# Where the gate's sigmoid is taken: moved from ScalarE's eviction to a pass over the reloaded gate, in a linear-attention layer on eight cores

## The reference, cut to what matters

```python
xn = layernorm(x)
# attention half, 16 heads of 128, blocks of 256 tokens
q, k, v = split(silu(xn @ w_qkv.T))
# per head, over the 8 blocks:
o_inter = (q * q_decay) @ kv
o_intra = ((q @ k.T) * diag_decay) @ v
kv      = block_decay * kv + (k * k_decay).T @ v
out  = norm_w * out * rsqrt(mean(out * out) + 1e-6)     # over all 2048 features
gate = sigmoid(xn @ w_gate.T)
s    = (gate * out) @ w_out.T
# weight of the second half, from 4 planes of 2048x2048 each
W    = sum_n (sigmoid(pw_n) - sigmoid(nw_n)) * c_n
g    = silu(xn @ W.T + bias)
y    = x + s * g
```

## Time and profile before

| | us |
|---|---|
| median of 2 runs | 2446.24 (2442.86 to 2449.62) |
| the profiled execution, whole | 2436.33 |
| its span, slowest core (core 5) | 2434.5 |
| spans of the 8 cores | 2415.6 to 2434.5 |
| busy on core 5: TensorE, VectorE, ScalarE | 1639.0, 868.0, 569.7 |

### The profile page before, as it was taken

One profiled execution on the slowest core, in us unless ns is written; L12 is line 12 of the kernel. 1 busy time (PEld: TensorE's weight loads), 2 busy tenths in 40 slices (PEclk: granted clock), 3 DMA queues, 4 the chain that ended last, 5 costly groups with the idle time before them and its releaser, 6 DMA issues.

```text
span 2434.5 us, 22652 instructions; the slowest of 8 cores (2415.6 to 2434.5 us)
## 1 busy us (share of the span) xinstructions
PE 1639.0 (67%) x7928; PEld 765.6 (31%) x7928; DVE 868.0 (36%) x1613; ACT 569.7 (23%) x827; POOL 191.1 (8%) x308
## 2 busy tenths in 40 slices
PE   1110545554459999288888888888888887357896
PEld 1110212221124444144344343434334343123332
DVE  5555254445550000223333333333333333623455
ACT  1225355555562122311111111111111111000000
POOL 0002232222220000000000000000000000110000
PEclk9999777776679999699999999999999998578998
DMA  8219899999991111122222212222222200697554
GB/s 190 101 55 121 118 158 154 155 162 161 152 156 37 39 37 56 23 27 44 44 44 44 35 30 32 35 44 44 44 44 44 44 18 9 130 190 168 169 166 154
DMA packets 176704, 211.74 MB, mean 87 GB/s; under 512 B 74064, under 2 KB 123216, under 8 KB 172496
## 3 DMA queue, kind: packets, MB, share of 16 engines
q0 software_dynamic: 135936, 109.07, 35.4%
q1 hardware_dynamic: 40656, 101.23, 12.7%
HBM read 277.37 MB, written 41.94 MB: 131 GB/s over the span
## 4 chain that ended last, share of the span: by engine, by line
PE 46%; DMA 27%; DVE 12%; issue 8%; ACT 5%; SPq 2%; DVEq 0%; POOL 0%; ACTq 0%; POOLq 0%
PE pfA L579 29%; DMA pnbg<-nwT 19%; DMA xT_fc<-xT 6%; PE pfA L452 5%; PE pS L452 5%; ACT sq_b L724 2%; DVE sT_b L675 2%; PE pT L611 2%; SPq L841 1%; DVE mneg_c L197 1%; DVE s L910 1%; DVE s L916 1%; PE pS L727 1%; DMA xtile<-x 1%; PE pS L663 1%
## 5 line engine op out<-in xcount | busy, mean ns | idle before, releaser
L579 PE MATMUL pfA<-xnT,wq_sb 128*128 128x512 bf16 x3072 | 721.4, 390 | 46.0 <-ACT q_dim L595 43.0
L579 PEld LDWEIGHTS pfA<-xnT,wq_sb 128*128 128x128 bf16 x3072 | 298.5, 100 | 404.5 <-issue 83.9
L354 PE MATMUL pfA<-xnT,wg_sb 128*128 128x512 bf16 x512 | 146.5, 457 | 307.1 <-ACT gate_stA L364 245.5
L675 DVE TENSOR_TENSOR sT_b<-pS,decT_all 128x512 bf16<-128x512 f32 x128 | 88.4, 690 | 317.6 <-PE pS L663 317.6
L406 DVE TENSOR_TENSOR sgp<-sgp,sgn 128x1024 bf16<-128x1024 bf16 x128 | 88.6, 692 | 269.8 <-ACT sgn L402 269.8
L354 PEld LDWEIGHTS pfA<-xnT,wg_sb 128*128 128x128 bf16 x512 | 57.1, 114 | 396.1 <-issue 358.4
L732 DVE SCALAR_TENSOR_TENSOR O_st<-pO,csb,gate_h 128x256 bf16<-128x256 f32 x128 | 61.9, 483 | 308.0 <-ACT sq_b L724 306.4
L397 ACT ACTIVATE sgp<-pnbg 128x1024 bf16<-128x1024 bf16 x128 | 135.2, 1056 | 133.5 <-DMA pnbg<-pwT 125.7
L402 ACT ACTIVATE sgn<-pnbg 128x1024 bf16<-128x1024 bf16 x128 | 135.1, 1056 | 91.5 <-DMA pnbg<-nwT 86.1
L901 PE MATMUL pfA<-O_sb,wout_sb 128*128 128x512 bf16 x512 | 125.7, 404 | 31.9 <-DVE s L910 31.9
L901 PE MATMUL pS<-O_sb,wout_sb 128*128 128x512 bf16 x512 | 119.7, 393 | 25.6 <-DMA O_sb<-o_scr 15.9
(11 more groups left out here) (106 smaller groups left out, 1491.9 us busy)
## 6 DMA issues: line engine op xcount, KB each, us to landing
pnbg<-pwT POOLq DMA_DIRECT2D x128, 256.0 KB, 14.1
pnbg<-nwT POOLq DMA_DIRECT2D x128, 256.0 KB, 13.2
wq_sb<-wqkvT POOLq DMA_DIRECT2D x16, 1536.0 KB, 19.2
xtile<-x SPq DMA_DIRECT2D x16, 1024.0 KB, 5.4
xT_fc<-xT SPq DMA_DIRECT2D x16, 1024.0 KB, 7.5
outT<-outb SPq DMA_DIRECT2D x64, 256.0 KB, 2.4
wg_sb<-wgateT POOLq DMA_DIRECT2D x16, 512.0 KB, 15.3
gate_scr<-gate_stA SPq DMA_DIRECT2D x16, 512.0 KB, 9.3
```

Source lines behind the costliest of these rows:

```text
L354: r = e.matmul(pbank[:], wg_sb[b][:, fc * HD:(fc + 1) * HD], xnT[:, fc * T + tg * 512: fc * T + tg * 512 + 512], start=(fc == 0), stop=(fc ...
L579: r = e.matmul(pfA[par][:], wq_sb[hb][:, fc * 384 + sel * 128: fc * 384 + (sel + 1) * 128], xnT[:, fc * T + tg * 512: fc * T + tg * 512 + ...
L675: tst = sch.op("V", (lambda h, jp: lambda e: e.tensor_tensor(out=sT_b[:, jp * 512:(jp + 1) * 512], in0=pS[jp][:], in1=decT_all[:, h * 512: ...
```

## The change

The eviction of the gate's matmuls in stage B moves from ScalarE to VectorE and becomes a plain copy; DRAM then holds the gate before its sigmoid. In stage C a sigmoid is taken in place over the whole tile `gate_h` (128x2048) on ScalarE, after each load: twice ahead of the loop (heads 0 and 1), and 14 times at a head boundary. The multiplication L732 waits for that instead of for the load.

```diff
-                tok_gst[h * NTG + tg] = sch.op("S",
-                    (lambda h, gb, tg, pbank: lambda e: e.activation(
-                        out=gate_st[gb][:, tg * 512:(tg + 1) * 512], in_=pbank[:],
-                        func=AF.Sigmoid))(h, gb, tg, pbank),
+                tok_gst[h * NTG + tg] = sch.op("V",
+                    (lambda h, gb, tg, pbank: lambda e: e.tensor_copy(
+                        out=gate_st[gb][:, tg * 512:(tg + 1) * 512],
+                        in_=pbank[:]))(h, gb, tg, pbank),
                     waits=[tok_gmm[(h, tg)], tok_gsd.get(h - 1)], inc=True)
...
+        tok_gsig[0] = sch.op("S", lambda e: e.activation(
+            out=gate_h[0][:], in_=gate_h[0][:], func=AF.Sigmoid),
+            waits=[tok_gld[0]], inc=True)
...
+            tok_gsig[1] = sch.op("S", lambda e: e.activation(
+                out=gate_h[1][:], in_=gate_h[1][:], func=AF.Sigmoid),
+                waits=[tok_gld[1]], inc=True)
...
                 waits=[tog, t_cst, tok_ost.get(h - 2), tok_sq[(h, j)],
-                       tok_gld[h]], inc=True)
+                       tok_gsig[h]], inc=True)
...
+                    tok_gsig[sh + 2] = sch.op("S",
+                        (lambda sh: lambda e: e.activation(
+                            out=gate_h[sh % 2][:], in_=gate_h[sh % 2][:],
+                            func=AF.Sigmoid))(sh),
+                        waits=[tok_gld[sh + 2]], inc=True)
```

More of the change, by code:

```diff
@@ L557, in build_program @@
         tok_wq[0] = tok_wq0
+        tok_gsig = {}
         tok_gld[0] = sch.op("Q", lambda e: e.dma_start(
```

## The result

The changed kernel takes **2481.95 us** (median of 11 runs, lowest 2475.12), the kernel before on the same chip 2449.55 (10 runs): ratio **1.0126**, 95% interval 1.0094 to 1.0158, some 31 us more. The forecast was 2480. (Medians are of all executions; the ratio and its interval compare undisturbed ones alone.)

What follows compares the result with a forecast made beforehand. Stage B's first half was taken as bound by its loads, stage C by TensorE's chain in program order. 3.7 + 5.2 + 20 + 5 = 34 us on the median of 2446.2 gave 2480 us, range 2459 to 2518.

Steps and rivals of the forecast that it cites:

- Part 1: Stage B's gate eviction as VectorE copies: TensorE restarts later behind the last chunk, +3.7 us.
- The cover at the other chunks: Stage B before the last chunk: later gate matmuls stay hidden, with 1.4 us of slack before GpSimd's next load; 0 us.
- Part 2: Two sigmoids ahead of stage C's loop, plus one more table switch, delay the first Silu: +5.2 us, bounds 3.9 and 5.5.
- Part 3: Fourteen sigmoids at stage C's head boundaries: landing, table loads and sigmoid delay the Square TensorE needs; +20 us, bounds 5 and 55.
- The clock: After boundary stalls in stage C, TensorE's granted clock falls for a second stretch: +5 us, bounds 0 and 14.
- The sum: All terms over the whole kernel: 34 us added to the median of 2446.2, giving 2480 us.
- in step to the end: Rival, stage C boundaries: two cores stay side by side, the slow one paying 54.7 us; 2523 us, chance 0.13.
- hidden: Rival, stage C boundaries: gate loads land quickly enough, boundaries cost 5 us in all; 2460 us, chance 0.12.
- Relief: Rival, stage B: taking 34.9 us of evictions off ScalarE shortens the loads; 2435 us, not slower, chance 0.08.
- A drain at every switch: Rival, stage C boundaries: each table switch back costs about 1.3 us extra, 28 to 36 us; near 2512 us, chance 0.05.

Runs made afterwards that it cites:

- the copy on VectorE alone: The kernel before with only the gate's eviction changed, to a copy on VectorE, and the gate's sigmoid left out: 2438.95 us, ratio 1.0034.
- The run with the weights a moment later: The changed kernel, with the next head's weights load also waiting for VectorE's last multiplication of the block (L739): 2459.04 us, ratio 1.0059.

## Why the prediction was right, step by step

- **Part 1, +3.7 us:** 3.6. The copy took 0.68 us, where the nearest row gave 0.69. The cover at the other chunks held but for short waits (2.3 us once on the core read above); the end of L424 does not show them.
- **Part 2, +5.2 us:** 5.0. The passes took 1.91 and 1.89 us, not 1.97. Exp's table did not hold Sigmoid: the switch is in the trace.
- **Part 3, +20 us:** 12.4 in waits. This is the term that was mis-sized. For a core out of step I had 15, a little too much too: before, the Square stood 12.3 to 12.4 us behind the issue at the nine slow boundaries of cores 1 and 5 and not 12.2, and the chain from the landing to it is 5.1 us and not 5.2. The rest of the 20 stood for cores 4 and 5 of the profiled execution, whose landings of 12 to 14 us were that execution's chance and not those cores' nature: in the changed kernel's profile they land as early as the others. The bounds of 5 and 55 held, and the reading that the stall drives such a pair apart was borne out by the table above.
- **The clock, +5 us:** 6.6, in the groups right behind the 14 waits. Behind waits of about 2 us most of them already took 5.3 us, mostly at the lower level; I had expected that of stalls of 6 us only. Where the waits went, these groups were at 3.63 us again.
- **The sum, 34 us:** 27.8 by stages, about 31 by the ratio. That the forecast of 2480 came within 2 us of the measured median is in part luck: part 3 was 7.6 us too high, and the median of the kernel before, on which the sum was put, came out 3 us higher with more runs.
- **The rivals:** *in step to the end* and *hidden* did not occur. *Relief* fell by three readings: end of L424 unchanged, ScalarE's waits for landings up by the 35 us that it was relieved of, and the ratio of the copy on VectorE alone above 1. *A drain at every switch* fell: table loads stand without a gap, and the 29 loads cost what their own 1.28 us cost.
- What I had not seen in the rows of before is why five of the 14 gate loads were quick. On every core of that trace four of them are issued only 0.26 to 0.51 us behind the weights' load, and beside the fifth, the last, no weights are loaded; the nine slow ones stand 0.75 us or more behind. The run with the weights a moment later shows that this distance is the cause.

## What to carry to other kernels

Work that moves to an engine with idle time is free only if, in that engine's order, nothing behind it is awaited: count from the event that the moved work waits for to the next result that the bounding engine needs, with the table loads on both sides, and compare that with the slack there. If the event is a DMA's landing, ask which larger load is issued just ahead of it; a shift of 0.87 us between two issues was worth 18 us here. And an engine with much idle time in total (ScalarE, 24% busy) can still hold the chain at one place: taking 25 us out of TensorE's wait of 43 us for the decay factors brought 26 us, nearly as much as the whole change cost.

## What the runs showed of the hardware that I had not expected

- A gate load of 512 KB lands about 5 us after its issue (means of 4.9 to 5.9 by core) when it is issued 0.1 us ahead of a 1.5 MB load on GpSimd's queue, and 8 us and more when it is issued 0.77 us behind it; 0.25 to 0.5 us behind, it still takes about 5.
- Two neighbouring cores that load at the same moment (within 3 us) need 10 us on average for the gate's load on the one and 8 on the other, against 7. The Trainium skill ("HBM Reference", Specifications) says that the two cores of a domain share its bandwidth, with which the pairs (0, 1), (4, 5) and (6, 7) agree; no run shows which cores share a memory.
- TensorE's granted clock fell to 0.58 behind a wait of 2.25 us that followed a sparse stretch, and that cost 1.7 us on the next group, nearly as much as the wait.
